# Attention stage: values weighted for two key tiles in every second step, row reciprocals spread through broadcast stationary columns, and three of sixteen evacuations done whole by ScalarE

## The chip, the core and the metric

The kernel runs on one core of a Trainium2 chip. The metric is device time in microseconds of one execution, as a median of several; a lower time is better. Engines are named as in the profile: PE is TensorE (PEld its loads of stationary data), DVE is VectorE, ACT is ScalarE, POOL is GpSimd, SP is SyncE.

## The reference

A chain of layers on x (2 x 512 x 1024): cross attention onto a context (2 x 1024 x 1024), a feed-forward layer, a quantised product, and a layer with Sinkhorn iterations. The change lies in the attention alone:

```python
query = query.reshape(b, N_KV_GROUPS, H_PER_G, n, D_HEAD)      # 2, 8, 4, 512, 32
scores = jnp.einsum('bghnd,bgsd->bghns', query, key) / D_HEAD ** 0.5
scores = jnp.where(mask, scores, jnp.finfo(scores.dtype).min)
attention = jax.nn.softmax(scores, axis=-1)                    # over 1024 keys
out = jnp.einsum('bghns,bgsd->bghnd', attention, value)
```

There are 16 pairs of batch and group, each with 4 heads, 512 queries, 1024 keys and heads of 32 values.

## The kernel before

Five stages run one after the other. Stage a makes queries, keys and values, stage b is the attention, stages c to e are the rest. Only `stage_b` is touched.

Stage b handles one of the 16 pairs of batch and group ("a group" below) in 16 steps: four tiles of 128 queries times four heads. Step k of 256 does the following.

- **Score**: PE multiplies 128 queries with 1024 keys into `psS` (two matmuls of 512 columns, L568). `psS` holds two steps, and the score is issued two steps ahead: step k issues `score(k+2)`.
- **Mask and minimum**: DVE adds the mask and takes the row minimum (L704, writes `Sc`, which holds four steps).
- **Exponentials**: ACT computes them with the row sums (L652, writes `Pr`).
- **Turn**: PE transposes the 1024 probabilities of each query tile as eight 128x128 blocks into `psT` (L618). `psT` has two halves of four blocks, f = 0 and f = 1, and holds one step: each half must have been copied out before the next step's transposes may fill it.
- **Keep**: ACT copies half 0 of `psT` to `PT` (L660), DVE copies half 1 (L713). The semaphores `kept[0]` and `kept[1]` tell PE.
- **Weigh**: for a unit of 8 steps (2 query tiles, 4 heads), PE multiplies the values with `PT`: eight key tiles, for each four heads side by side in the four 32-column strips of the array (L582). One key tile of the unit before is weighed in each step. In fp32 each of the four is two matmul instructions of 256 columns, so a key tile appears as x8.

At the end of a group the row sums are inverted on DVE (L717), turned on PE (L592, `turn_rec`, in step 10 of the next group), copied by ACT (L664), spread over the 32 rows of each head by a product with `headsel` (L598, `spread_rec`, step 13), and multiplied in by DVE (L724, `normalise`, step 15). `keep_O` (L670) copies the unscaled output out in step 8.

Each engine runs its own instructions strictly in the order in which the code issues them, and waits for the others through semaphores. In one step PE issues: score(k+2), transposes of half 0, weigh, transposes of half 1. DVE issues mask and minimum of k+2, then keep of k. ACT issues exponentials of k+1, then keep of k:

```python
for k in range(BODY):                 # DVE
    ...
    mask_min(it, k + 2, first)
    keep(it, k, first)
```

Of the kernel before, what the change touches and what calls it, by code (L numbers as in the profile page):

```python
# [25 lines left out]
ALU = mybir.AluOpType  # L26
# [4 lines left out]
P = 128  # L31
B, S, D = 2, 512, 1024
# [419 lines left out]
def stage_b(nc, mask, QHd, QLd, KHd, KLd, Vd, AOd, start_early_loads=None):  # L452
# [4 lines left out]
    with ExitStack() as stack:  # L457
# [10 lines left out]
        assert UNIT == NK  # L468
        ident = sb("b_ident", [P, P])
        headsel = sb("b_headsel", [HPG, P])  # L470
# [6 lines left out]
        Pr = sb("b_Pr", [P, 2, S2])  # L477
# [4 lines left out]
        recT = sb("b_recT", [HPG, S])  # L482
# [8 lines left out]
        selready = sem("b_selready")  # L491
# [13 lines left out]
        rec_turned = sem("b_recturned")  # L505
        recT_ready = sem("b_recT")
# [5 lines left out]
        QKV_DMAS = 9  # L512

# [46 lines left out]
        def _(pe):  # L560
# [11 lines left out]
            def weigh(it, k, first=False):  # L572

                u, unit, kt = (k // UNIT - 1) // 2 % 2, k // UNIT - 1, k % UNIT
                if kt == 0:
                    pe.wait_ge(kept[0], it * BODY + k)
                    pe.wait_ge(kept[1], it * BODY + k)
                    if unit % 2 == 0 and not first:
                        pe.wait_ge(AO_ready, it * 2 + (u - 1))
                cols = slice(unit % 2 * UQ, (unit % 2 + 1) * UQ)  # L580
                for h in range(HPG):
                    last = pe.matmul(psO[h * DH:(h + 1) * DH, u, cols], Vs[:, u, kt, :], PT[:, unit % 2, kt, h, :],  # L582
                                     start=(kt == 0), stop=(kt == NK - 1))
                if kt == NK - 1:
                    last.then_inc(weighed, 1)

            def turn_rec(bg, u):

                pe.wait_ge(rec_ready, bg + 1)
                pe.wait_ge(O_kept, bg + 1)  # L590
                for qt in range(QT):
                    last = pe.transpose(psO[0:HPG, u, qt * P:(qt + 1) * P], rec[:, u, qt * HPG:(qt + 1) * HPG],  # L592
                                        ident[:])
                last.then_inc(rec_turned, 1)

            def spread_rec(bg, u):
                pe.wait_ge(recT_ready, bg + 1)
                pe.matmul(psO[:, u, :], headsel[:], recT[:], start=True, stop=True).then_inc(spread, 1)  # L598

            def body(it, first=False, last=False):  # L600
                for k in range(BODY):
# [26 lines left out]
            pe.wait_ge(selready, 4)  # L628
# [10 lines left out]
            turn_rec(BG - 1, 1)  # L639
# [3 lines left out]
        def _(act):  # L643
            def exponentials(it, k, first=False):

                act.wait_ge(masked, it * BODY + (k + 1))
                if not (first and k < 2):
                    act.wait_ge(turned[1], it * BODY + (k - 1))
# [3 lines left out]
                act.activation(Pr[:, k % 2, :], Sc[:, k % 4, :], ACT.Exp, bias=mins[:, k % 4:k % 4 + 1], scale=-1.0,  # L652
                               accum_out=sums[:, u, j:j + 1]).then_inc(probs, 1)

            def keep(it, k, first=False):
                act.wait_ge(turned[0], it * BODY + (k + 1))
# [3 lines left out]
                act.copy(PT[:, (k // UNIT) % 2, 0:NK // 2, k % HPG, queries(k)], psT[:, 0, :, :]).then_inc(kept[0], 1)  # L660
# [11 lines left out]
            def body(it, first=False, last=False):  # L672
                for k in range(BODY):
# [6 lines left out]
                    if not (first and u == 0):  # L680
                        if j == UNIT:
                            keep_O(it * 2 + (u - 1), 1 - u, first and u == 1)
                        if j == UNIT + 4:
                            rec_rows(it * 2 + (u - 1), 1 - u)
# [8 lines left out]
            rec_rows(BG - 1, 1)  # L693

        @block.vector
        def _(dve):
# [11 lines left out]
            def keep(it, k, first=False):  # L708
                dve.wait_ge(turned[1], it * BODY + (k + 1))
# [16 lines left out]
            def body(it, first=False, last=False):  # L726
                for k in range(BODY):
# [29 lines left out]
        def _(pool):  # L757
            identity(pool, ident, setup)
            pool.memset(headsel[:], 1.0).then_inc(selready, 1)
            pool.wait_ge(selready, 1)  # L760
            pool.affine_select(out=headsel[:], in_=headsel[:], compare_op=ALU.is_ge, fill=0.0, base=0,
                               pattern=[[1, P]], channel_multiplier=-DH).then_inc(selready, 1)
            pool.wait_ge(selready, 2)
            pool.affine_select(out=headsel[:], in_=headsel[:], compare_op=ALU.is_ge, fill=0.0, base=DH - 1,
                               pattern=[[-1, P]], channel_multiplier=DH).then_inc(selready, 2)
# [1217 lines left out]
```

## Time and profile before

| | us |
|---|---|
| median of the runs | 1275.06 |
| span of the profiled execution, first to last instruction | 1275.0 |
| busy: PE, PEld, DVE, ACT, POOL | 1074.9, 748.7, 904.2, 670.6, 131.5 |
| first score of stage b to its last instruction on DVE, about | 242 to 802 |

The profiled execution's span and the median differ by less than 0.1 us, so nothing to speak of lies around the span. Times in rows are microseconds from the start of the span unless marked ns.

### The profile page before, as it was taken

Reading aid. Unit: us, or ns where it says so; the run is one execution under the profiler, and the core shown is the slowest. Engines: PE = TensorE matmul, PEld = TensorE weight load, DVE = VectorE, ACT = ScalarE, POOL = GpSimd, SP = SyncE. Lnnn points to the kernel's source line nnn. Section 1 sums busy time; section 2 is a strip of 40 time slices with the busy share of each in tenths; the row PEclk is TensorE's granted clock in tenths of the full one; section 3 lists DMA queues with packets and bytes.
Section 4 is the critical chain, followed back from the end, with each engine's and each line's share of the span. In section 5 each row is a group of like instructions: output and inputs, shape, how many; then the busy total and the mean of one; then the engine's idle time right before and its main releaser. Section 6 shows DMA issues by size and latency. Waiting matters only on the chain. (4 is left out here: it accounts for less than half of the span.)

```text
span 1275.0 us, 20748 instructions
## 1 busy us (share of the span) xinstructions
PE 1074.9 (84%) x6960; PEld 748.7 (59%) x6960; DVE 904.2 (71%) x1889; ACT 670.6 (53%) x1146; POOL 131.5 (10%) x107
## 2 busy tenths in 40 slices
PE   4999899499999999999999999689999967622208
PEld 3788777366666666666666666168888833411107
DVE  6445732598888898888888887535534336689998
ACT  3223310488888888888888887423222156543214
POOL 3111300000000000000000000000032045224300
PEclk8999999699999999999999999889999989855559
DMA  4777931952112222222222110563240000000003
GB/s 167 249 268 265 371 125 38 229 168 59 44 47 44 62 62 62 62 62 62 58 62 62 45 30 10 158 214 96 66 149 0 0 1 1 12 1 0 0 0 132
DMA packets 55719, 112.82 MB, mean 88 GB/s; under 512 B 7884, under 2 KB 21324, under 8 KB 55548
## 3 DMA queue, kind: packets, MB, share of 16 engines
q1 hardware_dynamic: 55084, 111.74, 28.6%
q8 instruction: 25, 0.41, 0.1%
q10 hardware_dynamic: 528, 0.52, 0.1%
q14 instruction: 18, 0.15, 0.0%
q0 software_dynamic: 64, 0.00, 0.0%
HBM read 83.99 MB, written 27.26 MB: 87 GB/s over the span
## 5 line engine op out<-in xcount | busy, mean ns | idle before, releaser
L652 ACT ACTIVATE b_Pr<-b_Sc,b_mins 128x1024 f32<-128x1024 f32 x256 | 294.5, 1150 | 94.8 <-PE b_psT L618 70.8
L704 DVE CUSTOM_DVE_ANT_0 b_Sc<-b_psS,b_mbias 128x1024 f32<-128x1024 f32 x256 | 312.3, 1220 | 28.5 <-PE b_psS L568 28.3
L618 PE MATMUL b_psT<-b_ident,b_Pr 128*128 128x128 f32 x2048 | 321.0, 280 | 0.9 <-ACT b_PT L660 0.2
L618 PEld LDWEIGHTS b_psT<-b_ident,b_Pr 128*128 128x128 f32 x2048 | 235.0, 141 | 140.3 <-issue 99.9
L713 DVE COPY b_PT<-b_psT 128x512 f32<-128x512 f32 x256 | 176.9, 691 | 42.6 <-PE b_psT L618 40.1
L568 PE MATMUL b_psS<-b_Ks,b_Qs 128*128 128x512 f32 x512 | 183.1, 439 | 17.5 <-DMA b_Qs<-QLd 14.4
L582 PE MATMUL b_psO<-b_PT,b_Vs 128*32 128x256 f32 x2048 | 162.2, 390 | 1.3 <-DVE b_PT L713 0.9
L660 ACT COPY b_PT<-b_psT 128x512 f32<-128x512 f32 x256 | 145.1, 567 | 13.8 <-PE b_psT L618 13.2
L568 PEld LDWEIGHTS b_psS<-b_Ks,b_Qs 128*128 128x128 f32 x512 | 78.3, 193 | 29.6 <-issue 25.2
L1039 ACT ACTIVATE c_sd<-c_mv,c_eps 128x1 f32<-128x1 f32 x16 | 4.7, 295 | 142.9 <-DVE c_mv L1121 142.9
L270 PE MATMUL a_psM<-XTh,WTh 128*128 128x512 f32 x192 | 75.7, 394 | 3.6 <-DVE WTl L345 3.6
L270 PE MATMUL a_psM<-XTh,WTl 128*128 128x512 f32 x192 | 75.2, 392 | 0.0
L270 PE MATMUL a_psM<-XTl,WTh 128*128 128x512 f32 x192 | 75.2, 392 | 0.0
L1114 DVE TENSOR_TENSOR XR<-XR,c_psM 128x1024 f32 (+1 forms) x16 | 19.5, 1221 | 75.4 <-PE c_psM L950 75.4
L582 PEld LDWEIGHTS b_psO<-b_PT,b_Vs 128*32 128x32 f32 x2048 | 42.0, 108 | 44.6 <-issue 43.7
L314 ACT ACTIVATE a_oh<-a_psM 128x512 fp32r<-128x512 f32 x24 | 14.4, 598 | 98.1 <-PE a_psM L270 91.9
L1615 PE MATMUL e_psT<-e_XN,e_dg 128*128 x128 | 30.0, 399 | 41.2 <-DVE XR L1870 41.2
L381 DVE SCALAR_TENSOR_TENSOR a_ol<-a_psM,a_oh 128x512 fp32r<-128x512 f32 x24 | 16.6, 691 | 64.9 <-ACT a_oh L314 64.9
L60 POOL MEMSET c_ident<- 128x128 f32 x1 | 0.2, 204 | 574.1 <-POOLq L457 574.1
L950 PE MATMUL c_psM<-WOh,c_Lh 128*128 128x512 f32 x128 | 51.8, 405 | 4.2 <-issue 4.2
L1615 PEld LDWEIGHTS e_psT<-e_XN,e_dg 128*128 128x128 f32 x128 | 25.7, 202 | 45.7 <-issue 41.9
L950 PE MATMUL c_psM<-WOh,c_Ll 128*128 128x512 f32 x128 | 51.8, 404 | 0.0
(219 smaller groups left out, 1673.0 us busy)
## 6 DMA issues: line engine op xcount, KB each, us to landing
a_xn<-in_ctx_turned SPq DMA_DIRECT2D x16, 512.0 KB, 3.4
XS<-in_ctx SPq DMA_DIRECT2D x16, 512.0 KB, 5.8
b_Qs<-QHd SPq DMA_DIRECT2D x30, 256.0 KB, 4.6
b_Qs<-QLd SPq DMA_DIRECT2D x30, 256.0 KB, 5.2
XS<-in_x SPq DMA_DIRECT2D x8, 512.0 KB, 10.2
a_wst<-in_L_xattn_w_q SPq DMA_DIRECT2D x8, 512.0 KB, 5.1
Q2d<-a_q SPq DMA_DIRECT2D x16, 256.0 KB, 4.7
QHd<-a_oh SPq DMA_DIRECT2D x16, 256.0 KB, 4.0
```

The lines of the kernel that those rows point to most:

```text
L270: last = pe.matmul(psM[:, slot, :], a[:, w_slot, k, :], m[:, k, cols], start=(k == 0 and a is WTh and m is mh), stop=(k == KT - 1 and a is ...
L381: dve.scalar_tensor_tensor(out=ol[:, slot, :], in0=psM[:, ps_slot, :], scalar=scale, in1=oh[:, slot, :].bitcast(F32), op0=ALU.mult, op1=AL ...
L568: last = pe.matmul(psS[:, k % 2, n * HALF:(n + 1) * HALF], Qs[:, u, h, qt * P:(qt + 1) * P], Ks[:, u, n * HALF:(n + 1) * HALF], start=True ...
L582: last = pe.matmul(psO[h * DH:(h + 1) * DH, u, cols], Vs[:, u, kt, :], PT[:, unit % 2, kt, h, :], start=(kt == 0), stop=(kt == NK - 1))
L618: last_t = pe.transpose(psT[:, f, t, :], Pr[:, k % 2, kt * P:(kt + 1) * P], ident[:])
L652: act.activation(Pr[:, k % 2, :], Sc[:, k % 4, :], ACT.Exp, bias=mins[:, k % 4:k % 4 + 1], scale=-1.0, accum_out=sums[:, u, j:j + 1]).then ...
L660: act.copy(PT[:, (k // UNIT) % 2, 0:NK // 2, k % HPG, queries(k)], psT[:, 0, :, :]).then_inc(kept[0], 1)
L704: dve.tensor_tensor_reduce(out=Sc[:, k % 4, :], in0=psS[:, k % 2, :], in1=mbias[:, qt, :], scale=1.0, scalar=3.4e38, op0=ALU.add, op1=ALU.min,
L713: dve.tensor_copy(PT[:, (k // UNIT) % 2, NK // 2:NK, k % HPG, queries(k)], psT[:, 1, :, :]).then_inc(kept[1], 1)
L950: last = pe.matmul(psM[:, u, cols], a[:, u, k, :], w[:, k, cols], start=(k == 0 and i == 0), stop=(k == KT - 1 and i == 2))
L1114: dve.tensor_tensor(row, row, psM[:, u, :], ALU.add).then_inc(added, 1)
L1615: last = pe.matmul(psX(u)[:, i * CH:(i + 1) * CH], dg[:, u, n, i, :], XN[:, ds(t, 1), n * CH:(n + 1) * CH].rearrange("p a n -> p (a n)"), ...
```

## The change

Six things change, all in stage b.

1. PE no longer weighs one key tile in each step between the two halves of the transposes. It weighs two key tiles (16 instructions) after the transposes of every odd step, and none in an even step.
2. In steps 2, 7 and 12 of each group (`WHOLE`) ACT copies all eight blocks of `psT` in one instruction once both halves are turned, and DVE copies nothing. `kept[0]` is then the signal for both halves, and `kept[1]` counts only the other 13 steps (`HALVED`, `halved(k)`).
3. `Pr` holds four steps instead of two, and the exponentials wait for the transposes of four steps before instead of two.
4. `turn_rec`, the ACT copy `rec_rows`, `recT` and `headsel` are gone. `spread_rec` now takes each column of reciprocals, repeated 32 times, as stationary operand against the identity: 16 matmuls of 128 columns in 32-column strips, in step 10.
5. `normalise` moves from step 15 to step 13.
6. POOL no longer prepares `headsel`.

```diff
+        PR = 4
+        WHOLE = (2, 7, 12)
+        HALVED = BODY - 2 * len(WHOLE)
-        headsel = sb("b_headsel", [HPG, P])
-        Pr = sb("b_Pr", [P, 2, S2])
+        Pr = sb("b_Pr", [P, PR, S2])
-        recT = sb("b_recT", [HPG, S])
+        def halved(k):
+
+            return sum(i % STEPS not in WHOLE for i in range(k))
@@ weigh
-                    pe.wait_ge(kept[1], it * BODY + k)
+                    pe.wait_ge(kept[1], it * HALVED + halved(k))
@@ turn_rec, spread_rec
-            def turn_rec(bg, u):
+            def spread_rec(bg, u):
 
                 pe.wait_ge(rec_ready, bg + 1)
                 pe.wait_ge(O_kept, bg + 1)
                 for qt in range(QT):
-                    last = pe.transpose(psO[0:HPG, u, qt * P:(qt + 1) * P], rec[:, u, qt * HPG:(qt + 1) * HPG],
-                                        ident[:])
-                last.then_inc(rec_turned, 1)
-
-            def spread_rec(bg, u):
-                pe.wait_ge(recT_ready, bg + 1)
-                pe.matmul(psO[:, u, :], headsel[:], recT[:], start=True, stop=True).then_inc(spread, 1)
+                    for h in range(HPG):
+                        one = rec[:, u, qt * HPG + h:qt * HPG + h + 1].to_broadcast([P, DH])
+                        last = pe.matmul(psO[h * DH:(h + 1) * DH, u, qt * P:(qt + 1) * P], one, ident[:],
+                                         start=True, stop=True)
+                last.then_inc(spread, 1)
@@ PE body
                     for f in range(2):
-                        if f == 1 and not (first and k < UNIT):
-                            weigh(it, k, first)
-                        if not (first and k == 0):
-                            pe.wait_ge(kept[f], it * BODY + k)
+                        if f == 1 and k and (k - 1) % STEPS not in WHOLE:
+                            pe.wait_ge(kept[1], it * HALVED + halved(k))
+                        elif f == 1 and k == 0 and not first:
+                            pe.wait_ge(kept[1], it * HALVED)
+                        elif f == 0 and not (first and k == 0):
+                            pe.wait_ge(kept[0], it * BODY + k)
                         for t in range(NK // 2):
                             kt = f * (NK // 2) + t
-                            last_t = pe.transpose(psT[:, f, t, :], Pr[:, k % 2, kt * P:(kt + 1) * P], ident[:])
+                            last_t = pe.transpose(psT[:, f, t, :], Pr[:, k % PR, kt * P:(kt + 1) * P], ident[:])
                         last_t.then_inc(turned[f], 1)
 
-                    if not (first and u == 0):
-                        if j == UNIT + 2:
-                            turn_rec(it * 2 + (u - 1), 1 - u)
-                        if j == UNIT + 5:
-                            spread_rec(it * 2 + (u - 1), 1 - u)
+                    if k % 2 == 1 and not (first and k < UNIT):
+                        weigh(it, k - 1, first)
+                        weigh(it, k, first)
+
+                    if j == UNIT + 2 and not (first and u == 0):
+                        spread_rec(it * 2 + (u - 1), 1 - u)
@@ ACT
-                if not (first and k < 2):
-                    act.wait_ge(turned[1], it * BODY + (k - 1))
+                if not (first and k < PR):
+                    act.wait_ge(turned[1], it * BODY + (k + 1 - PR))
             def keep(it, k, first=False):
-                act.wait_ge(turned[0], it * BODY + (k + 1))
+                whole = k % STEPS in WHOLE
+                act.wait_ge(turned[1 if whole else 0], it * BODY + (k + 1))
...
+                if whole:
+                    act.copy(PT[:, (k // UNIT) % 2, :, k % HPG, queries(k)],
+                             psT[:].rearrange("p f t n -> p (f t) n")).then_inc(kept[0], 1)
-            def rec_rows(bg, u):
-                act.wait_ge(rec_turned, bg + 1)
-                act.copy(recT[:], psO[0:HPG, u, :]).then_inc(recT_ready, 1)
@@ DVE
             def keep(it, k, first=False):
+                if k % STEPS in WHOLE:
+                    return
                 dve.wait_ge(turned[1], it * BODY + (k + 1))
@@
-                        if j == UNIT + 7:
+                        if j == UNIT + 5:
                             normalise(it * 2 + (u - 1), 1 - u, None if first else it * 16)
```

How the change moves instructions is shown at three places. The first is PE in steps 14 and 15 of a group. Before, step 14 and the start of step 15 (L568 score, L618 transposes, L582 weigh):

```order
L568 MATMUL b_psS<-b_Ks,b_Qs 128x512 [waits b_qkv1,b_masked]
L568 MATMUL b_psS<-b_Ks,b_Qs 128x512
L618 MATMUL b_psT<-b_ident,b_Pr 128x128 [waits b_kept0,b_probs]
L618 MATMUL b_psT<-b_ident,b_Pr 128x128 x3
L582 MATMUL b_psO<-b_PT,b_Vs 32x256 x4
L618 MATMUL b_psT<-b_ident,b_Pr 128x128 [waits b_kept1]
L618 MATMUL b_psT<-b_ident,b_Pr 128x128 x3
L568 MATMUL b_psS<-b_Ks,b_Qs 128x512 [waits b_masked]
L568 MATMUL b_psS<-b_Ks,b_Qs 128x512
```

After, from the second score matmul of step 14 to the end of step 15 (L570 score, L620 transposes, L584 weigh):

```order
L570 MATMUL b_psS<-b_Ks,b_Qs 128x512
L620 MATMUL b_psT<-b_ident,b_Pr 128x128 [waits b_kept0,b_probs]
L620 MATMUL b_psT<-b_ident,b_Pr 128x128 x3
L620 MATMUL b_psT<-b_ident,b_Pr 128x128 [waits b_kept1]
L620 MATMUL b_psT<-b_ident,b_Pr 128x128 x3
L570 MATMUL b_psS<-b_Ks,b_Qs 128x512 [waits b_masked]
L570 MATMUL b_psS<-b_Ks,b_Qs 128x512
L620 MATMUL b_psT<-b_ident,b_Pr 128x128 [waits b_kept0,b_probs]
L620 MATMUL b_psT<-b_ident,b_Pr 128x128 x3
L620 MATMUL b_psT<-b_ident,b_Pr 128x128 [waits b_kept1]
L620 MATMUL b_psT<-b_ident,b_Pr 128x128 x3
L584 MATMUL b_psO<-b_PT,b_Vs 32x256 x8
```

The weigh of step 14 has left its place between the halves and stands with that of step 15 behind all transposes; the second half of each step, which waits for `b_kept1`, now follows the first half at once.

The second place is PE at the end of step 10, the turn of the reciprocals before:

```order
L618 MATMUL b_psT<-b_ident,b_Pr 128x128 [waits b_kept1]
L618 MATMUL b_psT<-b_ident,b_Pr 128x128 x3
L592 MATMUL b_psO<-b_ident,b_rec 4x128 [waits b_Okept,b_rec]
L592 MATMUL b_psO<-b_ident,b_rec 4x128 x3
L568 MATMUL b_psS<-b_Ks,b_Qs 128x512 [waits b_masked]
L568 MATMUL b_psS<-b_Ks,b_Qs 128x512
```

and the same place after, where the spread itself stands (L596) and step 10 has no weigh:

```order
L620 MATMUL b_psT<-b_ident,b_Pr 128x128 [waits b_kept1]
L620 MATMUL b_psT<-b_ident,b_Pr 128x128 x3
L596 MATMUL b_psO<-b_ident,b_rec 32x128 [waits b_Okept,b_rec]
L596 MATMUL b_psO<-b_ident,b_rec 32x128 x15
L570 MATMUL b_psS<-b_Ks,b_Qs 128x512 [waits b_masked]
L570 MATMUL b_psS<-b_Ks,b_Qs 128x512
```

The third place is ACT in steps 1 to 3 of a group, before (L652 exponentials, L660 keep):

```order
L660 COPY b_PT<-b_psT 128x4x128 [waits b_turned0]
L646 REGISTER_ALU
L652 ACTIVATE b_Pr,b_sums<-b_Sc,b_mins 128x1024 [waits b_turned1,b_masked]
L660 COPY b_PT<-b_psT 128x4x128 [waits b_turned0]
L646 REGISTER_ALU
L652 ACTIVATE b_Pr,b_sums<-b_Sc,b_mins 128x1024 [waits b_turned1,b_masked]
L660 COPY b_PT<-b_psT 128x4x128 [waits b_turned0]
```

and after (L653, L666 keep of a half, L663 keep of all eight blocks):

```order
L666 COPY b_PT<-b_psT 128x4x128 [waits b_turned0]
L647 REGISTER_ALU
L653 ACTIVATE b_Pr,b_sums<-b_Sc,b_mins 128x1024 [waits b_turned1,b_masked]
L663 COPY b_PT<-b_psT 128x8x128 [waits b_turned1]
L647 REGISTER_ALU
L653 ACTIVATE b_Pr,b_sums<-b_Sc,b_mins 128x1024 [waits b_turned1,b_masked]
L666 COPY b_PT<-b_psT 128x4x128 [waits b_turned0]
```

Both begin with the keep of step 1. The keep of step 2 now waits for the second half of the transposes and moves eight blocks. On DVE, after, the same place reads mask of step 3, keep of step 1, masks of steps 4 and 5, keep of step 3 (L704 mask and minimum, L715 keep):

```order
L704 ISA b_Sc,b_mins<-b_psS,b_mbias 128x1024 [waits b_scored,b_probs]
L704 ISA b_mins 128x1
L715 COPY b_PT<-b_psT 128x4x128 [waits b_turned1]
L704 ISA b_Sc,b_mins<-b_psS,b_mbias 128x1024 [waits b_scored,b_probs]
L704 ISA b_mins 128x1
L704 ISA b_Sc,b_mins<-b_psS,b_mbias 128x1024 [waits b_scored,b_probs]
L704 ISA b_mins 128x1
L715 COPY b_PT<-b_psT 128x4x128 [waits b_turned1]
```

What moved on DVE is only this: the keep (L715) of step 2 is gone from between two masks.

## Rows read from the trace of the kernel before

**Rows 1.** The page, 40 slices of the span: TensorE and its granted clock, in tenths

```profile
PE   4999899499999999999999999689999967622208
...
PEclk8999999699999999999999999889999989855559
```

**Rows 2.** Windows, one stretch of stage b: PE, PEld, DVE, ACT, POOL busy, PEclk

```profile
433.00:466.00 33.00, 32.92 (x279) 21.15 (x280) 29.14 (x49) 26.73 (x48) 0.00 (x0) 1.00 0.26 60
```

**Rows 3.** Timeline, two steps from 514.7 us: start, duration, engine, line, operands, idle before

```profile
514.75 0.71 PE L568 MATMUL b_psS<-b_Ks,b_Qs 128*128 128x512 f32 x2
...
515.30 0.60 PE L618 MATMUL b_psT<-b_ident,b_Pr 128*128 128x128 f32 x4
...
515.83 0.64 PE L582 MATMUL b_psO<-b_PT,b_Vs 128*32 128x256 f32 x8
...
516.40 0.66 PE L618 MATMUL b_psT<-b_ident,b_Pr 128*128 128x128 f32 x4
...
516.81 0.71 PE L568 MATMUL b_psS<-b_Ks,b_Qs 128*128 128x512 f32 x2
...
517.10 0.69 DVE L713 COPY b_PT<-b_psT 128x512 f32<-128x512 f32 x1
...
517.37 0.60 PE L618 MATMUL b_psT<-b_ident,b_Pr 128*128 128x128 f32 x4
...
518.50 0.33 PE L618 MATMUL b_psT<-b_ident,b_Pr 128*128 128x128 f32 x1
```

**Rows 4.** The page, costliest groups: busy us, mean ns of one, idle before

```profile
L582 PE MATMUL b_psO<-b_PT,b_Vs 128*32 128x256 f32 x2048 | 162.2, 390 | 1.3 <-DVE b_PT L713 0.9
```

**Rows 5.** Timeline of 254 to 257.5 us, steps that weigh nothing yet

```profile
254.12 0.69 DVE L713 COPY b_PT<-b_psT 128x512 f32<-128x512 f32 x1
...
254.72 1.22 DVE L704 CUSTOM_DVE_ANT_0 b_Sc<-b_psS,b_mbias 128x1024 f32<-128x1024 f32 x1
...
255.28 0.71 PE L568 MATMUL b_psS<-b_Ks,b_Qs 128*128 128x512 f32 x2
...
255.39 0.56 ACT L660 COPY b_PT<-b_psT 128x512 f32<-128x512 f32 x1
...
255.86 0.69 DVE L713 COPY b_PT<-b_psT 128x512 f32<-128x512 f32 x1
...
256.10 1.17 PE L618 MATMUL b_psT<-b_ident,b_Pr 128*128 128x128 f32 x8
```

**Rows 6.** Timeline of 504.4 to 513.9 us, the steps with L592 and L598

```profile
504.42 0.66 PE L618 MATMUL b_psT<-b_ident,b_Pr 128*128 128x128 f32 x4
...
505.27 0.71 PE L568 MATMUL b_psS<-b_Ks,b_Qs 128*128 128x512 f32 x2
...
506.20 1.23 DVE L704 CUSTOM_DVE_ANT_0 b_Sc<-b_psS,b_mbias 128x1024 f32<-128x1024 f32 x1 [0.40 <-PE b_psS L568]
...
511.03 0.66 PE L618 MATMUL b_psT<-b_ident,b_Pr 128*128 128x128 f32 x4
...
512.67 0.73 PE L568 MATMUL b_psS<-b_Ks,b_Qs 128*128 128x512 f32 x2
...
513.68 1.22 DVE L704 CUSTOM_DVE_ANT_0 b_Sc<-b_psS,b_mbias 128x1024 f32<-128x1024 f32 x1 [1.26 <-PE b_psS L568]
```

**Rows 7.** Timeline of TensorE, L592 in two groups that stand two groups apart

```profile
435.48 0.27 PE L592 MATMUL b_psO<-b_ident,b_rec 128*4 128x128 f32 x1
...
504.91 0.27 PE L592 MATMUL b_psO<-b_ident,b_rec 128*4 128x128 f32 x1
```

**Rows 8.** ScalarE's groups by line and shape: busy us, mean ns, idle before

```profile
L1035 ACT ACTIVATE c_Lh<-c_psT 128x1024 fp32r<-128x1024 f32 x8 | 8.2, 1020 | 0.3
...
L1315 ACT COPY d_q1T<-d_psB 128x1024 bf16<-128x1024 bf16 x8 | 8.0, 996 | 3.6 <-PE d_psB L1265 3.5
```

**Rows 9.** Timeline of 798 to 812 us, the end of stage b

```profile
799.02 0.60 PE L592 MATMUL b_psO<-b_ident,b_rec 128*4 128x128 f32 x4 [0.79 <-ACT b_Os L670]
...
801.44 0.69 DVE L724 TENSOR_TENSOR b_AOs<-b_psO,b_Os 128x512 f32<-128x512 f32 x1 [6.26 <-PE b_psO L598]
```

More of the change, by code:

```diff
@@ L490, in stage_b @@
         setup = sem("b_setup")
-        selready = sem("b_selready")
         mask_in = sem("b_mask_in")
@@ L504, in stage_b @@
         rec_ready = sem("b_rec")
-        rec_turned = sem("b_recturned")
-        recT_ready = sem("b_recT")
         spread = sem("b_spread")
@@ L611, in body @@
                     for f in range(2):
-                        if f == 1 and not (first and k < UNIT):
-                            weigh(it, k, first)
-                        if not (first and k == 0):
-                            pe.wait_ge(kept[f], it * BODY + k)
+                        if f == 1 and k and (k - 1) % STEPS not in WHOLE:
[4 more added lines that the diff above has]
+                            pe.wait_ge(kept[0], it * BODY + k)
                         for t in range(NK // 2):
                             kt = f * (NK // 2) + t
-                            last_t = pe.transpose(psT[:, f, t, :], Pr[:, k % 2, kt * P:(kt + 1) * P], ident[:])
+                            last_t = pe.transpose(psT[:, f, t, :], Pr[:, k % PR, kt * P:(kt + 1) * P], ident[:])
                         last_t.then_inc(turned[f], 1)
-                    if not (first and u == 0):
-                        if j == UNIT + 2:
-                            turn_rec(it * 2 + (u - 1), 1 - u)
-                        if j == UNIT + 5:
-                            spread_rec(it * 2 + (u - 1), 1 - u)
+                    if k % 2 == 1 and not (first and k < UNIT):
[3 more added lines that the diff above has]
+                        spread_rec(it * 2 + (u - 1), 1 - u)
             pe.wait_ge(setup, 2)
-            pe.wait_ge(selready, 4)
             pe.wait_ge(first_in, 16 * 8)
@@ L638, in _ @@
                 weigh(BG // 2, k)
-            turn_rec(BG - 1, 1)
             spread_rec(BG - 1, 1)
@@ L651, in exponentials @@
                     act.wait_ge(rec_ready, it * 2 + (u - 1))
-                act.activation(Pr[:, k % 2, :], Sc[:, k % 4, :], ACT.Exp, bias=mins[:, k % 4:k % 4 + 1], scale=-1.0,
+                act.activation(Pr[:, k % PR, :], Sc[:, k % 4, :], ACT.Exp, bias=mins[:, k % 4:k % 4 + 1], scale=-1.0,
                                accum_out=sums[:, u, j:j + 1]).then_inc(probs, 1)
             def keep(it, k, first=False):
-                act.wait_ge(turned[0], it * BODY + (k + 1))
+                whole = k % STEPS in WHOLE
+                act.wait_ge(turned[1 if whole else 0], it * BODY + (k + 1))
                 if not (first and k < 2 * UNIT):
@@ L659, in keep @@
                         act.wait_ge(weighed, it * (BODY // UNIT) + (k // UNIT - 1))
-                act.copy(PT[:, (k // UNIT) % 2, 0:NK // 2, k % HPG, queries(k)], psT[:, 0, :, :]).then_inc(kept[0], 1)
-            def rec_rows(bg, u):
-                act.wait_ge(rec_turned, bg + 1)
-                act.copy(recT[:], psO[0:HPG, u, :]).then_inc(recT_ready, 1)
+                if whole:
+                    act.copy(PT[:, (k // UNIT) % 2, :, k % HPG, queries(k)],
+                             psT[:].rearrange("p f t n -> p (f t) n")).then_inc(kept[0], 1)
+                else:
+                    act.copy(PT[:, (k // UNIT) % 2, 0:NK // 2, k % HPG, queries(k)], psT[:, 0, :, :]
+                             ).then_inc(kept[0], 1)
             def keep_O(bg, u, first=False):
@@ L682, in body @@
                             keep_O(it * 2 + (u - 1), 1 - u, first and u == 1)
-                        if j == UNIT + 4:
-                            rec_rows(it * 2 + (u - 1), 1 - u)
             act.dma_start(mk8[:], mask.rearrange("(t p) k -> p t k", p=P)).then_inc(mask_in, 16)
@@ L692, in _ @@
             keep_O(BG - 1, 1)
-            rec_rows(BG - 1, 1)
         @block.vector
@@ L758, in _ @@
             identity(pool, ident, setup)
[L759 to L765, printed above, removed]
 class EarlyLoads:
```

## Prediction

> **What bounds the kernel now.** The 40 slices of the page come first. From about 255 to 800 us, where stage b runs, TensorE is busy 99% and its clock is granted in full, the 2.4 GHz level [rows 1]. The table by windows confirms it for one stretch: PE 32.92 us of 33, DVE 29.14, ACT 26.73 [rows 2]. So each step ends when PE has issued its instructions. The timeline shows what a step consists of [rows 3]: score to transposes .55 us (514.75 to 515.30), transposes of half 0 to weigh .53, weigh to transposes of half 1 .57, transposes to score .41. Together 2.06 us a step. Two groups, 32 steps, take 504.91 - 435.48 = 69.43 us, or 34.72 a group [rows 7]; 16 x 2.06 = 32.96 of it are plain steps, and the rest are the two insertions [rows 6]: with L592 transposes to score take .85 instead of .41 (+.44), with L598 1.64 instead of .41 (+1.23).
>
> What PE does not show is how far behind it the others are. That is read where PE is not the limit: the first steps of stage b weigh nothing, and there DVE repeats a cycle of 1.74 us [rows 5]: keep to mask .60 (254.12 to 254.72), mask to the next keep 1.14 (254.72 to 255.86). There, too, a keep on DVE holds up the transposes of half 1, and the score that follows starts 1.16 us after the keep (254.12 to 255.28). Since score follows transposes by .41 in this form, the transposes themselves start .75 after the keep started. These three numbers are the latencies of the loop through DVE.
>
> **What the change removes from PE.** Transposes are spaced .11 us (a group of four lasts .60, one alone .27 [rows 3, 7]), so four take .44. A key tile is two rounds of four strips; its eight last .64 [rows 3] and one .39 [rows 4], so the second round starts .24 to .25 after the first. I take .24, and .48 a tile. A turn to the narrow strips and back costs .53 - .44 = .09, .57 - .48 = .09, and .06 in the next group (.66 against .60): .24 us. Weighing two tiles at once saves one turn in two steps, so a pair of steps would take 2 x 2.06 - .24 = 3.88 us if nothing waited. DVE's 1.74 us a step and ACT's load [rows 2] lie below the 1.94 that this makes, so on averages the change looks like a gain.
>
> The Trainium skill (TensorEngine Tiling, Key Properties) says that changing the tiling mode drains TensorE. The trace agrees with the .24 us. By that rule alone the sum is the first rival below.
>
> **What it puts in place of it.** The order within a pair decides. Take an even step k. PE issues score(k+2) only after the double weigh of the step before. DVE's next instruction is the mask of k+2, and keep(k) is queued behind it. The transposes of half 1 in step k+1 wait for keep(k) (`kept[1]`), and behind them on PE stand the double weigh and score(k+4), which the next even mask needs. This is a closed loop:
>
> - score(k+2) to mask: .93 after a plain change of work (505.27 to 506.20, DVE idle before), 1.01 in another place (512.67 to 513.68) [rows 6]. I take .95.
> - mask to keep(k): 1.14 [rows 5].
> - keep(k) to transposes of half 1 of step k+1: .75 [rows 5].
> - these to the weigh: .53 + .06, since transposes that waited have the long form (.66 instead of .60 [rows 3]): .59.
> - double weigh to score(k+4): one tile takes .57, two .57 + .48 = 1.05.
>
> Sum 4.48 us a pair, against 3.88 that PE needs and 4.12 that two steps take now. Without any wait PE would reach those transposes .55 + .44 + .35 + .55 + .44 = 2.33 us after the score, but keep(k) lets them go only after .95 + 1.14 + .75 = 2.84: PE waits .51 us in each pair, about (.60 in all with the longer forms). In the kernel before the same distance is from 514.75 to 518.50, 3.75 us [rows 3], against the same 2.84: .9 us in hand, because the weigh stood between and each step had one. `Pr` with four buffers does not help here: the exponentials are not in the loop. Where an exponential waits for transposes today, the wait costs nothing.
>
> **The three whole evacuations.** DVE gains nothing in the loop by them: step 7 is odd, and there DVE has idle time anyway, waiting for the next score. In steps 2 and 12 keep(k) on DVE is gone, so its loop is cut, but now the transposes of half 0 of the next step wait for ACT. From score(k+2): .55 + .44 to the transposes of half 1, .60 + .04 to their copy (517.06, when the group of 516.40 ends, to 517.10 [rows 3]), the copy of 1024 columns from PSUM 1.00 to 1.02 by two like instructions [rows 8], .15 to the transposes (255.39 + .56 to 256.10 [rows 5]), .44 to half 1: 3.23 instead of 2.84. Less .06 for the form, and rounded: +.35 us, twice a group. After step 7 the double weigh and a score (1.6 us) stand between and cover the 1.2 us of the copy: 0. If the copy took only .8 or as much as 1.3 us, the term would be +.15 or +.65.
>
> **The reciprocals.** L592 and L598 leave PE (.44 + 1.23, inside the 34.72). The new spread is 32 instructions, eight rounds of four strips with half the columns of a weigh. Nothing in the trace is quite like it. The bounds are .12 (half of .24) and .24 us a round; I take .14, near the lower, as the columns halve. 8 x .14 + .09 = 1.21 to the score of step 11, after .53 from the transposes. From score(12) the transposes of half 1 of step 11 then start at .55 + .44 + .53 + 1.21 + .55 + .44 = 3.72 instead of 2.84; less .06, +.82 us once a group (+.66 to +1.6 by the bounds). It stands in an even step, where part of it covers the wait. `normalise` two steps earlier and DVE's reciprocals fall into DVE's idle time before a score: 0. At the very end the spread follows alone: before, 799.02 to 801.44 = 2.42 us from L592 to the product [rows 9]; after, 1.12 + .2 = about 1.3, so -1.1 us. POOL's preparation lies before stage b's data arrive: 0. No DMA is moved, and the loads of the next group have a longer group to hide in.
>
> **The sum.** The new cadence holds from step 8 of the first group to the end, 248 steps or 15.5 groups: 124 pairs x 4.48 = 555.5; 31 whole copies x .35 = 10.9; 15 spreads x .82 = 12.3; together 578.7. Before: 15.5 x 34.72 = 538.2. Difference +40.5, with the end +39.4. The first eight steps stay with DVE, 0. The profiled span and the median are alike (1275.0 and 1275.06), so **1314.5 us**, 3.1% slower.
>
> **Rivals.**
>
> *The keep is hidden after all* and PE stays the bound, as the averages and the rule of drains suggest. 124 x 3.88 = 481.1. The whole copies then show fully: half 0 could start at .55 + .44 + .35 + .55 = 1.89 and may at 2.79, .90 x 31 = 27.9. Spreads 15 x (1.21 + .09) = 19.5. Sum 528.5, less 538.2, less 1.1: 1264 us, .8% faster. For it: 99% busy on PE, 88% on DVE. It decides as soon as score to transposes-let-go falls from 2.84 to 2.33, and no latency I read leaves room for .5 us. 10%. If the whole copies were hidden too, 1236 us, 3% faster: 3%.
>
> *Part of the loop is shorter*, say 4.25 us a pair, because waits on different engines overlap more than where I read them: 124 x .23 = 29 us less, 1286 us. 9%.
>
> *The clock falls.* PE would idle .6 of 4.48 us. Further on a slice with PE at 7 tenths has a clock of 9 tenths, and two at 6 have 8 [rows 1]. At the 1.2 GHz level at least the transposes and weighs in the loop would double, .33 + .96 us a pair, 160 us in all: 1475 us. 2%.
>
> **How the numbers follow.** Forecast 1314.5 us, chance 76%. Its own range: the loop between 4.40 and 4.60 (-10 to +15 us, mainly score to mask and entering the score after a weigh), whole copies -6 to +9, spreads -2 to +12: about 1300 to 1335. For 8 in 10 the range reaches down towards the partial case: 1292 to 1336. A measurement of this kernel can tell about 2% from no change, that is below 1249.6 and above 1300.6. Faster: 4%. Same: 10 + most of the 9 + the lower edge of the forecast = 18%. Slower: 78%.
>
> **What the profile after would show.** In stage b pairs of 4.4 to 4.6 us from one double weigh to the next; PE idle about half a microsecond before the second transposes of every odd step, released by DVE's keep (L715); PE near 87% busy there, the clock still full; DVE idle before each even mask, released by the score; before step 3 and step 13 PE waiting for ACT's L663 of about 1.0 us; L596 about 1.2 us once a group; stage b some 40 us longer, everything behind it as long as before. A pair of 3.9 us with PE 99% busy would mean the first rival, and would show that a keep can run before the mask it is queued behind, or that one of the three latencies is not what the quiet steps show.

## Result and profile after

The changed kernel takes 1308.49 us against 1275.03 us, medians of four runs each. The ratio is 1.0258, with a 95% interval of 1.0240 to 1.0276: slower by 2.6%. The prediction said 1314.5 us, 3.1% slower. One execution of the kernel before (2187.14 us) and one of e7 below (3204.01 us) took far longer than all others, and no ratio counts them.

The page of the changed kernel, first TensorE and its clock over the span in 40 slices, then the two groups in which the change shows most (busy us, mean ns of one, idle before and its releaser):

```profile
PE   4999897599999999999999999769999977622208
...
PEclk8899999799999999999999999879999989865559
...
L704 DVE CUSTOM_DVE_ANT_0 b_Sc<-b_psS,b_mbias 128x1024 f32<-128x1024 f32 x256 | 311.8, 1218 | 132.0 <-ACT b_Pr L653 71.9
L620 PE MATMUL b_psT<-b_ident,b_Pr 128*128 128x128 f32 x2048 | 286.8, 277 | 46.2 <-ACT b_PT L663 24.0
```

The clock is much as before [rows 1]. By windows it is at its 1.2 GHz level (granted .50) where stage b starts, up to about 245 us in the kernel before and 247 us here, and at 1.00 from 248 us to the end of the stage. PE still reads 9 tenths in stage b, so the slices hide the loss. It shows in the idle columns: PE stood 46 us before the transposes (24 of them for ACT's whole copies), and DVE 132 us before its masks, against 28.5 us before the masks in the kernel before. The table by windows for 170 us of stage b, columns as in [rows 2]:

```profile
300.00:470.00 170.00, 156.35 (x1476) 106.11 (x1474) 129.05 (x217) 135.61 (x225) 0.00 (x0) 1.00 0.25 58
```

PE is busy 92% here against 99.8% in [rows 2], DVE 76% against 88%. The timeline of one pair of steps, from the score that opens it to the next such score, is the main reading (start, duration, engine, line, operands, idle before):

```profile
498.83 0.73 PE L570 MATMUL b_psS<-b_Ks,b_Qs 128*128 128x512 f32 x2
...
499.78 1.23 DVE L704 CUSTOM_DVE_ANT_0 b_Sc<-b_psS,b_mbias 128x1024 f32<-128x1024 f32 x1 [0.85 <-ACT b_Pr L653]
...
500.19 0.70 PE L570 MATMUL b_psS<-b_Ks,b_Qs 128*128 128x512 f32 x2
...
500.84 0.63 PE L620 MATMUL b_psT<-b_ident,b_Pr 128*128 128x128 f32 x4
...
500.93 0.69 DVE L715 COPY b_PT<-b_psT 128x512 f32<-128x512 f32 x1
...
501.67 0.42 PEld L620 LDWEIGHTS b_psT<-b_ident,b_Pr 128*128 128x128 f32 x4 [0.44 <-DVE b_PT L715]
501.67 0.66 PE L620 MATMUL b_psT<-b_ident,b_Pr 128*128 128x128 f32 x4 [0.21 <-DVE b_PT L715]
...
502.26 1.07 PE L584 MATMUL b_psO<-b_PT,b_Vs 128*32 128x256 f32 x16
...
503.26 0.73 PE L570 MATMUL b_psS<-b_Ks,b_Qs 128*128 128x512 f32 x2
```

Read as the loop of the prediction: score 498.83, mask 499.78 (.95), keep 500.93 (1.15), second transposes 501.67 (.74), double weigh 502.26 (.59), next score 503.26 (1.00). Sum 4.43 us. Before the transposes at 501.67 the weight loads (PEld) stand .44 us idle, released by DVE's keep. In [rows 3] the same transposes follow a weigh and wait for nothing.

One thing in this fence misleads. The profile puts DVE's idle time before the mask down to ACT's exponentials. The mask waits for two semaphores, the score and the exponentials of four steps before, and those exponentials had ended more than a pair of steps earlier. The mask starts .95 us after its score here, .95 at 447.50 to 448.45 below, and .93 in [rows 6]: it waits for the score.

The timeline of the pair with the new spread, of the whole evacuation in step 12 that follows, of the score and mask behind it, and the double weigh one group later:

```profile
446.50 1.07 PE L584 MATMUL b_psO<-b_PT,b_Vs 128*32 128x256 f32 x16
...
447.50 0.73 PE L570 MATMUL b_psS<-b_Ks,b_Qs 128*128 128x512 f32 x2
...
448.45 1.22 DVE L704 CUSTOM_DVE_ANT_0 b_Sc<-b_psS,b_mbias 128x1024 f32<-128x1024 f32 x1 [0.85 <-ACT b_Pr L653]
...
449.03 1.08 PE L596 MATMUL b_psO<-b_ident,b_rec 128*32 128x128 f32 x32
...
450.04 0.73 PE L570 MATMUL b_psS<-b_Ks,b_Qs 128*128 128x512 f32 x2
...
451.58 0.59 PEld L584 LDWEIGHTS b_psO<-b_PT,b_Vs 128*32 128x32 f32 x16 [0.17 <-issue]
...
454.22 1.01 ACT L663 COPY b_PT<-b_psT 128x1024 f32<-128x1024 f32 x1 [0.71 <-PE b_psT L620]
...
455.38 1.06 PE L620 MATMUL b_psT<-b_ident,b_Pr 128*128 128x128 f32 x8 [0.73 <-ACT b_PT L663]
...
456.37 0.59 PEld L584 LDWEIGHTS b_psO<-b_PT,b_Vs 128*32 128x32 f32 x16 [0.17 <-issue]
...
457.37 0.73 PE L570 MATMUL b_psS<-b_Ks,b_Qs 128*128 128x512 f32 x2
...
458.38 1.23 DVE L704 CUSTOM_DVE_ANT_0 b_Sc<-b_psS,b_mbias 128x1024 f32<-128x1024 f32 x1 [0.62 <-PE b_psS L570]
...
483.52 1.07 PE L584 MATMUL b_psO<-b_PT,b_Vs 128*32 128x256 f32 x16
```

The spread takes 449.03 to 450.04, 1.01 us up to the next score, and this pair lasts 451.58 - 446.50 = 5.08 us. Then the whole evacuation: second transposes of step 12, ACT's copy 454.22 to 455.23, next transposes 455.38, and PE idle .73 us on ACT. This pair lasts 456.37 - 451.58 = 4.79; of the .73 us of wait only .36 make it longer than 4.43. In the pair behind it the mask starts 1.01 us after its score (457.37 to 458.38), and that pair lasts 4.49. This group is 483.52 - 446.50 = 37.02 us against 34.72 in [rows 7]; the next is 36.81, the mean 36.93.

Who waited for whom from 300 to 820 us (us in total, times, longest), and below it the end of the stage:

```profile
DVE b_Sc L704 <- ACT b_Pr L653: 67.2, 85, 0.9
...
DVE b_Sc L704 <- PE b_psS L570: 45.5, 42, 1.5
...
PEld b_psT L620 <- DVE b_PT L715: 36.4, 70, 0.9
ACT b_PT L663 <- PE b_psT L620: 20.7, 28, 0.8
PE b_psT L620 <- ACT b_PT L663: 20.4, 28, 0.7
PE b_psT L620 <- DVE b_PT L715: 19.8, 70, 0.6
```

```profile
834.31 1.08 PE L596 MATMUL b_psO<-b_ident,b_rec 128*32 128x128 f32 x32 [0.79 <-ACT b_Os L673]
835.45 0.69 DVE L726 TENSOR_TENSOR b_AOs<-b_psO,b_Os 128x512 f32<-128x512 f32 x1 [5.57 <-PE b_psO L596]
```

From the spread's start to the product it is now 1.14 us against 2.42 [rows 9]. Stage b ends at 835.45 instead of 801.44, 34.0 us later; .7 of that are there already where PE starts to work without long waits (scores at 242.13 us instead of 241.45), so the stage from there on is 33.3 us longer. The span of this execution is 1311.3 us, 36.3 more than before; it was the slowest of the four (1313.04 us, the others 1306.57 to 1308.8), and 2.3 us of it lie behind stage b, where no instruction changed.

### The profile page after: what moved, and what is told of

Read it like the earlier page. It is cut to its first block and busy times, and to the rows that moved or that the text cites. A ratio compares the mean times of both kernels' runs of the same rounds, so it can differ in the third digit from the quotient of the medians.

```text
span 1311.3 us, 21665 instructions
## 1 busy us (share of the span) xinstructions
PE 1065.6 (81%) x7376; PEld 762.2 (58%) x7376; DVE 865.5 (66%) x1841; ACT 690.0 (53%) x1130; POOL 125.9 (10%) x104
## 5 line engine op out<-in xcount | busy, mean ns | idle before, releaser
L704 DVE CUSTOM_DVE_ANT_0 b_Sc<-b_psS,b_mbias 128x1024 f32<-128x1024 f32 x256 | 311.8, 1218 | 132.0 <-ACT b_Pr L653 71.9
L620 PE MATMUL b_psT<-b_ident,b_Pr 128*128 128x128 f32 x2048 | 286.8, 277 | 46.2 <-ACT b_PT L663 24.0
L653 ACT ACTIVATE b_Pr<-b_Sc,b_mins 128x1024 f32<-128x1024 f32 x256 | 295.0, 1152 | 55.5 <-DVE b_mins L704 52.8
L620 PEld LDWEIGHTS b_psT<-b_ident,b_Pr 128*128 128x128 f32 x2048 | 229.7, 141 | 122.0 <-issue 62.6
L570 PE MATMUL b_psS<-b_Ks,b_Qs 128*128 128x512 f32 x512 | 186.3, 446 | 17.2 <-DMA b_Qs<-QLd 14.0
L715 DVE COPY b_PT<-b_psT 128x512 f32<-128x512 f32 x208 | 142.9, 687 | 13.2 <-PE b_psT L620 13.1
L666 ACT COPY b_PT<-b_psT 128x512 f32<-128x512 f32 x208 | 120.2, 578 | 43.5 <-PE b_psT L620 43.2
L584 PE MATMUL b_psO<-b_PT,b_Vs 128*32 128x256 f32 x2048 | 136.3, 385 | 0.0
L570 PEld LDWEIGHTS b_psS<-b_Ks,b_Qs 128*128 128x128 f32 x512 | 77.7, 191 | 71.5 <-issue 55.0
L584 PEld LDWEIGHTS b_psO<-b_PT,b_Vs 128*32 128x32 f32 x2048 | 54.1, 109 | 43.3 <-issue 21.2
L663 ACT COPY b_PT<-b_psT 128x1024 f32<-128x1024 f32 x48 | 48.6, 1013 | 24.4 <-PE b_psT L620 23.2
```

The source lines that it names most:

```text
L570: last = pe.matmul(psS[:, k % 2, n * HALF:(n + 1) * HALF], Qs[:, u, h, qt * P:(qt + 1) * P], Ks[:, u, n * HALF:(n + 1) * HALF], start=True ...
L620: last_t = pe.transpose(psT[:, f, t, :], Pr[:, k % PR, kt * P:(kt + 1) * P], ident[:])
L653: act.activation(Pr[:, k % PR, :], Sc[:, k % 4, :], ACT.Exp, bias=mins[:, k % 4:k % 4 + 1], scale=-1.0, accum_out=sums[:, u, j:j + 1]).the ...
L663: act.copy(PT[:, (k // UNIT) % 2, :, k % HPG, queries(k)], psT[:].rearrange("p f t n -> p (f t) n")).then_inc(kept[0], 1)
L704: dve.tensor_tensor_reduce(out=Sc[:, k % 4, :], in0=psS[:, k % 2, :], in1=mbias[:, qt, :], scale=1.0, scalar=3.4e38, op0=ALU.add, op1=ALU.min,
L715: dve.tensor_copy(PT[:, (k // UNIT) % 2, NK // 2:NK, k % HPG, queries(k)], psT[:, 1, :, :]).then_inc(kept[1], 1)
```

## Experiments

Ratios are to the kernel before, run beside each experiment on the same chip (medians of 1276.8 to 1277.7 us there); intervals are 95%. The ratios are those on record, which differ from the quotient of the medians by up to .0013. e1 to e4, e5 to e8 and e9 to e11 ran on three chips, so across these sets the ratios and the traces are the surer comparison.

**e1: no whole evacuations.** Edit on the changed kernel:

```diff
-        WHOLE = (2, 7, 12)
+        WHOLE = ()
```

> The changed kernel with WHOLE = (), so ACT and DVE evacuate one half each in every step; all else as changed. Theory (the loop score, mask, keep, second transposes, double weigh sets the pair, and a whole evacuation only adds a wait for ACT in steps 2 and 12): pairs stay at 4.43 us, the two pairs of 4.79 become 4.43, 31 x .36 = 11 us less than the changed kernel, about 1297 us. Rival (the whole evacuations relieve DVE, which is the limit): without them the time rises, above 1308 us.

Measured 1300.13 us, ratio 1.0170 (1.0146 to 1.0195). In its trace the pairs of 4.79 are 4.43, the others unchanged, and a group is 36.16 us instead of 36.93. That is 12 us for 15.5 groups. The ratio moves by .0088, 11 us. The whole evacuations cost; they relieve nothing, since DVE sits idle before each even mask.

**e2 and e3: double weigh between the halves.** In e2 the pair of weighs moves ahead of the second half in odd steps, in e3 also `WHOLE = ()`:

```diff
                     for f in range(2):
+                        if f == 1 and k % 2 == 1 and not (first and k < UNIT):
+                            weigh(it, k - 1, first)
+                            weigh(it, k, first)
                         if f == 1 and k and (k - 1) % STEPS not in WHOLE:
...
-                    if k % 2 == 1 and not (first and k < UNIT):
-                        weigh(it, k - 1, first)
-                        weigh(it, k, first)
```

> The changed kernel, but the double weigh of an odd step stands between its two halves of transposes instead of behind them; WHOLE stays. Theory (place, not doubling, costs): keep(k) has the 1.0 us of the weigh more to arrive, the wait of .5 us goes, pairs near 3.83 to 3.88 us, but all three whole evacuations now show with about .9 us each: 34.4 us a group against 36.9, about 1270 us. Rival (two key tiles in one go cost by themselves, wherever they stand): stays above 1300 us.

> Both at once: double weigh between the halves of odd steps, WHOLE = (). Theory: PE is the bound again, pairs of 3.83 to 3.88 us, the spread adds about 1.1 us a group, 31.8 to 32.2 us a group against 34.7 before, so 1228 to 1237 us, faster than both kernels. Rival (DVE's own work is the limit once PE is quicker): pairs of 4.1 us or more, 1270 us.

Measured: e2 1296.17 us, ratio 1.0155 (1.0138 to 1.0172); e3 1254.26 us, ratio .9814 (.9794 to .9835). Both are faster than the changed kernel, as the theory said, and e3 beats both kernels with the same double weigh; e2 stays slower than the kernel before, where the theory had it faster. The sizes missed: e2 by 26 us, e3 by 17 us from the slow end of its range. A timeline of e3, steps from an even one on (PE, DVE, ACT as above):

```profile
504.07 0.59 PEld L584 LDWEIGHTS b_psO<-b_PT,b_Vs 128*32 128x32 f32 x16 [0.17 <-issue]
...
504.45 1.15 ACT L652 ACTIVATE b_Pr<-b_Sc,b_mins 128x1024 f32<-128x1024 f32 x1 [1.12 <-DVE b_mins L703]
...
505.07 0.66 PE L623 MATMUL b_psT<-b_ident,b_Pr 128*128 128x128 f32 x4
...
505.48 0.71 PE L570 MATMUL b_psS<-b_Ks,b_Qs 128*128 128x512 f32 x2
...
506.30 1.07 PE L623 MATMUL b_psT<-b_ident,b_Pr 128*128 128x128 f32 x8
...
507.12 0.71 PE L570 MATMUL b_psS<-b_Ks,b_Qs 128*128 128x512 f32 x2
...
508.52 1.07 PE L584 MATMUL b_psO<-b_PT,b_Vs 128*32 128x256 f32 x16
```

From weigh to weigh, 504.07 to 508.52, this pair at the start of a group lasts 4.45 us. Only the pair with the spread is longer, 5.13; most are 3.93, not 3.83 (two steps of the kernel before take 4.11 to 4.12, so the double weigh does save time in this place). Two things were left out. In an even step nothing stands between the two rounds of transposes but a score. Such a step takes 1.44 us where PE needs 1.36; the copy of one step (.31 to .36 after the last transpose's start, .75 to the next transposes) can account for .05 to .08 us, but no run tests it. And the first pair of a group is long because `normalise` and the reciprocals push a mask back; e7 tests that. The whole evacuations in e2 add 36.10 - 33.17 = 2.9 us a group, .98 each on average, where .9 was expected.

**e4: the double weigh alone.** The kernel before with

```diff
                     for f in range(2):
-                        if f == 1 and not (first and k < UNIT):
-                            weigh(it, k, first)
                         if not (first and k == 0):
                             pe.wait_ge(kept[f], it * BODY + k)
...
+                    if k % 2 == 1 and not (first and k < UNIT):
+                        weigh(it, k - 1, first)
+                        weigh(it, k, first)
```

> The kernel before with one edit, the double weigh behind the transposes of odd steps; single-half evacuations, two buffers of Pr and L592, L598 as before. Theory: this edit alone makes the loop, pairs of 4.43 us; L592 in an even step hides in the wait, L598 (1.2 us) in an odd step shows: 36.6 us a group, about 1305 us. Rival (the cost comes from the whole evacuations and the new spread, the double weigh saves its turns): below 1265 us.

Measured 1304.15 us, ratio 1.0216 (1.0194 to 1.0238). Pairs of 4.43, a group of 36.56 us where 36.6 was expected. This part of the change is enough for most of the loss; e11 shows that another part is enough as well.

**e5: two buffers of probabilities.** `PR = 4` becomes `PR = 2` in the changed kernel.

> The changed kernel with PR = 2, so exponentials wait for the transposes of two steps before as in the kernel before. Theory (the exponentials are not in the loop): no change, within .3% of the changed kernel, 1.02 to 1.03 of the kernel before. Rival (the deeper Pr already gives back part of the loss): 1.04 or more of the kernel before.

Measured 1309.74 us, ratio 1.0254 (1.0224 to 1.0284), the changed kernel's own. The deeper buffer buys nothing.

**e6: the new spread alone.** In the kernel before, `turn_rec`, `rec_rows` and the product with `headsel` give way to the changed `spread_rec` in step 10:

```diff
                         if j == UNIT + 2:
-                            turn_rec(it * 2 + (u - 1), 1 - u)
-                        if j == UNIT + 5:
                             spread_rec(it * 2 + (u - 1), 1 - u)
```

> The kernel before with the new reciprocal spread alone (L592 and L598 replaced by 32 narrow instructions in step 10, no copy on ACT, normalise still in step 15). Theory: 1.67 us a group leave PE, .20 to enter, eight rounds in .81 and .21 to leave come, less the .03 between transposes and score: 1.19. 15 groups x .48 = 7 us and 1 us at the end less, ratio .993 to .994. Rival (the narrow spread costs as much as what it replaces): ratio 1.000.

Measured 1267.09 us, ratio .9930 (.9902 to .9958). This part of the change gains .7%.

**e7: DVE's extras ahead of a keep that waits.** Edit on e3:

```diff
-                    keep(it, k, first)
                     if not (first and u == 0):
-                        if j == 0:
+                        if j == 1:
                             reciprocals(it * 2 + (u - 1), 1 - u)
                         if j == UNIT + 5:
                             normalise(it * 2 + (u - 1), 1 - u, None if first else it * 16)
+                    keep(it, k, first)
```

> e3 (double weigh between the halves, WHOLE = ()) with DVE's two extras ahead of a keep that waits anyway: reciprocals before keep of step 1 instead of behind keep of step 0, normalise before keep of step 13. Theory (the long pairs 0/1 in e3, 4.43 us against 3.93, come from masks pushed late by normalise and reciprocals): the pair falls to about 3.95, .5 to .6 us a group, 8 to 10 us less than e3, ratio .974 to .976. Rival (the long pair comes from the change of group itself, as loads of queries or weights of another group): no change, .981.

Measured 1251.13 us, ratio .9796 (.9761 to .9832). The pair at a group's start, 4.38 or 4.47 us in e3, fell to 3.96 us, so the extras were its cause. But the pair around step 13 rose from 3.93 to 4.12, and a group shrank only from 33.17 to 32.89 us, half of what was expected. The intervals of e3 and e7 overlap; in the medians the gain is 3 us.

**e8: keep before mask on DVE.** Edit on e1:

```diff
+                    keep(it, k, first)
                     if k + 2 < BODY:
                         mask_min(it, k + 2, first)
                     elif not last:
                         mask_min(it + 1, k + 2 - BODY)
-                    keep(it, k, first)
```

> e1 (changed, WHOLE = ()) with DVE's order turned: keep(k) before the mask of k+2, all else as in e1. Theory (the loop exists because keep is queued behind a mask that waits for the score after the double weigh): that loop is cut, and the next one decides: mask to exponentials 1.26, these to transposes 1.30, two halves and the copy 1.08, keep to mask .60, so 4.24 us for two steps against 4.43, about 34.3 us a group, 1270 to 1280 us. Rival (the second transposes wait for the duration of the copy wherever it is queued, or the double weigh itself costs): no change from e1, 1300 us.

Measured 1349.19 us, ratio 1.0566 (1.0534 to 1.0597): slower than e1 by some 50 us, where both theories had it level or faster. Waits (300 to 780 us) and timeline of e8:

```profile
ACT b_Pr L653 <- DVE b_mins L704: 137.5, 197, 1.1
DVE b_PT L715 <- PE b_psT L620: 109.3, 179, 1.0
PEld b_psT L620 <- ACT b_Pr L653: 90.4, 85, 1.2
PE b_psT L620 <- ACT b_PT L666: 56.0, 85, 0.8
```

```profile
512.15 1.21 DVE L704 CUSTOM_DVE_ANT_0 b_Sc<-b_psS,b_mbias 128x1024 f32<-128x1024 f32 x1
...
513.40 1.15 ACT L653 ACTIVATE b_Pr<-b_Sc,b_mins 128x1024 f32<-128x1024 f32 x1 [0.83 <-DVE b_mins L704]
...
513.71 1.07 PE L584 MATMUL b_psO<-b_PT,b_Vs 128*32 128x256 f32 x16
513.82 0.69 DVE L715 COPY b_PT<-b_psT 128x512 f32<-128x512 f32 x1 [0.45 <-PE b_psT L620]
...
514.43 1.21 DVE L704 CUSTOM_DVE_ANT_0 b_Sc<-b_psS,b_mbias 128x1024 f32<-128x1024 f32 x1
...
514.55 0.57 ACT L666 COPY b_PT<-b_psT 128x512 f32<-128x512 f32 x1
...
515.28 0.93 PE L620 MATMUL b_psT<-b_ident,b_Pr 128*128 128x128 f32 x7
```

The loop through DVE's queue is cut indeed: no transposes wait for DVE any more. Another took its place, and the expectation's sum had left out a part of it. The keep of half 0 on ACT stands behind the exponentials of the next step, exactly as DVE's keep stood behind a mask. Chain of one step: mask 512.15, exponentials 513.40 (1.25), ACT's keep 514.55 (1.15), next transposes 515.28 (.73), their copy on DVE and the next mask. With first to second half .44, second half to its copy .64, keep to mask .60 that is 4.81 us in two steps; the trace has 4.82. The expectation left out ACT's keep, .56 us.

**e9 and e10: the score ahead of the double weigh.** e9 is e1 with the score that opens an even step issued before the weighs of the odd step ahead of it (`next_score(it, k, last)` is the wait for `masked` and the score as they stood in the body):

```diff
-                    if not (last and k + 2 >= BODY):
-                        pe.wait_ge(masked, it * BODY + (k + 1))
-                        ...
+                    if k % 2 == 1 or (first and k == 0):
+                        next_score(it, k, last)
...
+                    if k % 2 == 1:
+                        next_score(it, k + 1, last)
                     if k % 2 == 1 and not (first and k < UNIT):
                         weigh(it, k - 1, first)
                         weigh(it, k, first)
```

> e1 (changed, WHOLE = ()) with one move on PE: the score that opens an even step is issued before the double weigh of the odd step ahead of it instead of behind. The double weigh stays behind the transposes and DVE's order stays. Theory (the double weigh costs because it stands inside the loop score, mask, keep, second transposes): the loop shrinks to .95 + 1.14 + .75 + .36 = 3.2 us, below PE's own 3.83, PE is the bound again, pairs 3.85 to 3.95 us, 32.2 to 33 us a group against 36.16 in e1, ratio .970 to .980. Rival (a double weigh of 1.0 us in one piece starves DVE and ACT wherever the score stands): stays above 4.2 us a pair, ratio above 1.00.

> e9 with DVE's extras placed before a keep of an even step: reciprocals in step 2, normalise in step 12. Theory: they fall into time in which DVE waits for transposes, .2 to .5 us a group less than e9, ratio .003 lower. Rival (DVE has no such time in e9): no change or slower.

Measured: e9 1245.51 us, ratio .9764 (.9742 to .9787), the fastest of the study; e10 1248.55 us, ratio .9787 (.9766 to .9808), no gain. Timeline of e9:

```profile
500.70 0.70 PE L570 MATMUL b_psS<-b_Ks,b_Qs 128*128 128x512 f32 x2
...
501.29 0.69 DVE L721 COPY b_PT<-b_psT 128x512 f32<-128x512 f32 x1
...
501.33 1.07 PE L584 MATMUL b_psO<-b_PT,b_Vs 128*32 128x256 f32 x16
...
501.89 1.22 DVE L710 CUSTOM_DVE_ANT_0 b_Sc<-b_psS,b_mbias 128x1024 f32<-128x1024 f32 x1
...
502.34 1.09 PE L624 MATMUL b_psT<-b_ident,b_Pr 128*128 128x128 f32 x8
...
503.19 0.71 PE L570 MATMUL b_psS<-b_Ks,b_Qs 128*128 128x512 f32 x2
...
503.84 1.13 PE L624 MATMUL b_psT<-b_ident,b_Pr 128*128 128x128 f32 x8
```

The double weigh is still one piece behind the transposes, 501.33 to 502.34. But DVE has its score at 500.70 and starts the mask at 501.89, while PE weighs. Most pairs are 3.93 us (those with the spread, `normalise` and the reciprocals 5.04, 4.13 and 4.02), and a group is 32.9 against 36.16 in e1. This is the sharpest test of the loop: the same work, the same order on DVE and ACT, one score ahead of 1.0 us of weighing instead of behind it, and some 50 us off e1. In e10 the pair with `normalise` takes 4.23 instead of 4.13 for another: DVE had no free time there.

**e11: whole evacuations with a weigh in each step.** In the changed kernel the weigh goes back to one tile a step between the halves (the inverse of e4's edit).

> The changed kernel with one key tile weighed in each step between the halves, as in the kernel before; whole evacuations, four buffers of Pr and the new spread stay. So it is e6 plus the whole evacuations. Theory (a whole evacuation makes the next transposes wait: .33 + .31 + 1.01 + .15 = 1.80 us from the last transposes' start instead of .91): .89 us in each of 48 steps, 43 us over e6, ratio 1.026. Rival (with a weigh in every step PE's slack hides them, and DVE gains): ratio .99 to 1.00.

Measured 1310.29 us, ratio 1.0271 (1.0251 to 1.0291). Steps 3, 8 and 13, each behind a whole evacuation, take 2.98 us from score to score instead of 2.06. With PE as the bound each costs .92, in the changed kernel only .36, because there the loop had a wait anyway. Against e6, which has no whole evacuations, that is 43 us, as expected. So the parts do not add up: the double weigh alone costs 28 us (e4), the whole evacuations alone 43, and both together with the spread only 33, since their waits overlap. Putting the single weigh back into the changed kernel gains nothing (1.0271 against 1.0258) as long as the whole evacuations stay.

## Why the prediction was right

- **What bounds it.** PE before, a loop through three engines after. Shown by e4 (the double weigh alone gives 4.43 us a pair), e3 and e9 (the same double weigh elsewhere, or the score elsewhere, gives 3.93), e8 (the wait for DVE vanishes when the keep is no longer queued behind the mask).
- **The loop, 4.48 us.** Measured 4.43. The first four links came as read to .01 us (.95, 1.15, .74, .59), the two taken from the first steps of the kernel before among them; the double weigh to the score took 1.00, not 1.05, since rounds behind the second follow in .22 instead of .24 us.
- **Whole evacuations, .35 us each in steps 2 and 12, 0 in step 7.** Measured .36, and 0 (the pair of step 7 is 4.43). e1 gives 12 us for all, the term said 11.
- **The spread, .82 us.** Measured 5.08 - 4.43 = .65. The term was mis-sized: it took .14 us a round and .09 to leave; eight rounds last .81 in all to the last one's start, and the score comes 1.01 after the spread's start instead of 1.21. The lower bound of .66, at .12 a round, was the right end.
- **The end, -1.1 us.** Measured 1.14 instead of 2.42, -1.3.
- **The sum.** With measured terms 124 x 4.43 + 31 x .36 + 15 x .65 = 570.2, less 538.2 and 1.3: +30.7 us, and +39.4 was forecast. The medians differ by 33.5. Of the other 2.8 us, .65 lie in the first eight steps, put at 0: 16.22 us from the scores at 242.13 to the score issued in step 8 instead of 15.57. The whole copies are not the reason, since e1 without them takes 16.18. The clock fits: from the same scores on it stays at the 1.2 GHz level some 1.5 us longer than in the kernel before (the third block of scores lasts 1.20 us instead of .93); why was not tested. Another 1.7 lie in pairs that last 4.48 to 4.53 us instead of 4.43 (one 4.78), up to three in every second group. One of these shows a mask .06 us later after its score; why only every second group has them is not settled. So the forecast stood 6 us too high, mainly through 124 x .05 of the loop and 15 x .17 of the spread; the terms put at 0 went the other way.
- **Profile after.** Right: idle time before the second transposes on DVE's keep, the clock, L663 at 1.01 us. Wrong: PE at 87%, it reads 92%. The matmuls before the wait are drawn to within .21 us of the late ones, though the weight loads stand .44 us, so only .21 us counts as idle PE. And the profile names ACT as the releaser of the even mask, not the score.
- **Rivals.** Hidden keeps would have given 1264 us. They are real in another order: e3 and e9, without whole evacuations, have the pairs that the first rival described, with 3.93 in place of 3.88 us. A loop of 4.25 us did not come, nor were the whole copies in steps 2 and 12 hidden. The clock stayed at its 2.4 GHz level (granted 1.00) from 248 us to the end of stage b, with PE busy 92%.

## What to carry to other kernels

Two engines at 88% and 81% beside one at 99% say how much work there is, not how late it may come. Before work is gathered into larger pieces on the busy engine, sum the loop of hand-overs that runs through that piece, with every instruction queued ahead on each engine (the e8 sum failed for exactly one of these), and compare it with the engine's own time. If the loop is longer, issue what starts the loop (here the score) ahead of the large piece. And do not add up what the parts of such a change cost by themselves: e4 by itself explains most of the loss, and e11 by itself all of it.

The latencies of such a loop can be read in a stretch where the bound engine is not the bound: here the first eight steps, which weigh nothing.

## Unexpected on the hardware

Column strips queue better than one pair of rounds shows. Four rounds of four fp32 strips with 256 columns follow at .24, .22 and .22 us, and eight rounds with 128 columns at about .115 us each, although every instruction loads 32 stationary columns that take .109 us by themselves (L596 in the changed kernel: 32 loads, the last round .81 us after the first). A stationary operand read as one column repeated 32 times loads as fast as a real one: .109 us for both L596 and L584.
